# Splitting an expert layer's weights during the attention ahead of it, packing the expert numbers, and 16 places for returned rows

## What is computed

```python
x = x + L0_attn(layernorm(x)); x = x + L0_xattn(layernorm(x), ctx, ctx, mask); x = x + L0_ffn(layernorm(x))
x = x + L1_attn(layernorm(x)); x = x + L1_xattn(layernorm(x), ctx);            x = x + L1_ffn(layernorm(x))
```

```python
Q = (query @ Wq).reshape(b, q_len, G, Hpg, dh) / sqrt(dh);  K = key @ Wk;  V = value @ Wv      # L0_xattn
scores = einsum('bqghd,bkgd->bghqk', Q, K) + m * rel         # masked where mask is false
out = einsum('bghqk,bkgd->bqghd', softmax(scores), V) @ Wo

aff = sigmoid(x @ wa);  p, i = top_k(aff, 2);  p = p / p.sum()                                  # L0_ffn
expert(x) = (gelu(x @ g + gb) * (x @ w1 + b1)) @ w2 + b2     # g, w1: 256 x 128; w2: 128 x 256
y = x + sum over the 2 shared experts + sum over the token's 2 chosen experts of p * expert(x)
```

## Time and profile before

| | |
|---|---|
| median of 3 runs | 2768.86 us (2767.92 to 2770.44) |
| the profiled execution | 2787.7 us, of which the profile shows a span of 2785.9 us |
| busy share of the span | TensorE 74%, VectorE 62%, ScalarE 51%, GpSimd 37% |
| cross attention with its norm | 258 to 475 us |
| norm and routing of the changed expert layer | 475 to 547 us |
| its routed experts | 547 to 694 us |
| shared experts, rows brought back | 694 to 748 us |

### The profile page before, as it was taken

One profiled execution on the slowest core, in us unless ns is written; L12 is line 12 of the kernel. 1 busy time (PEld: TensorE's weight loads), 2 busy tenths in 40 slices (PEclk: granted clock), 3 DMA queues, 4 the chain that ended last, 5 costly groups with the idle time before them and its releaser, 6 DMA issues. The chain is left out here.

```text
span 2785.9 us, 44119 instructions
## 1 busy us (share of the span) xinstructions
PE 2048.7 (74%) x15822; PEld 1226.0 (44%) x15822; DVE 1738.1 (62%) x3146; ACT 1420.1 (51%) x1986; POOL 1018.9 (37%) x920
## 2 busy tenths in 40 slices
PE   6783776156489999999856366666666549999998
PEld 3332554145267777777645122222222234444444
DVE  6996565612533333333365899999999645666665
ACT  4562333412143333333233488888888525666664
POOL 0000221641422322323223588888888600101010
PEclk9996777568789999999967555555555569999999
DMA  3000001576200000000000256666666400000001
GB/s 91 0 0 20 1 0 36 143 143 117 72 20 20 19 19 19 9 19 19 1 23 0 45 107 108 108 108 107 107 107 107 72 18 12 23 24 18 25 17 39
DMA packets 374723, 135.44 MB, mean 49 GB/s; under 512 B 317549, under 2 KB 371525, under 8 KB 374597
## 3 DMA queue, kind: packets, MB, share of 16 engines
q1 hardware_dynamic: 370757, 123.27, 21.8%
q0 software_dynamic: 3840, 10.49, 1.7%
HBM read 47.69 MB, written 10.49 MB: 21 GB/s over the span
## 5 line engine op out<-in xcount | busy, mean ns | idle before, releaser
L2015 POOL CAST xnT<-xl 128x2048 bf16<-128x2048 uint8 x256 | 484.0, 1891 | 15.5
L2050 PE MATMUL psum<-e_KT,e_QT 48*128 48x512 bf16 x1024 | 264.7, 617 | 272.0 <-DVE ctxT L2083 124.9
L2083 DVE TENSOR_SCALAR_CACHE_REDUCE ctxT<-psum,e_nsq 128x1024 f32<-128x1024 f32 x256 | 314.7, 1281 | 11.5 <-PE psum L2050 10.1
L2083 DVE TENSOR_SCALAR_CACHE_REDUCE e_Smore<-psum,e_nsq 128x1024 f32<-128x1024 f32 x256 | 314.7, 1281 | 1.7 <-issue 0.4
L2101 ACT ACTIVATE xh<-e_Smore,e_ebias 128x2048 uint8<-128x2048 f32 x128 | 256.3, 2002 | 48.8 <-POOL e_ebias L2022 48.8
L2101 ACT ACTIVATE xh<-ctxT,e_ebias 128x2048 uint8<-128x2048 f32 x128 | 256.3, 2002 | 47.2 <-POOL e_ebias L2022 47.2
L1563 POOL TENSOR_TENSOR d_sq<-d_oS 128x512 f32<-128x512 f32 x64 | 99.2, 1549 | 420.5 <-ACT d_oS L1607 420.5
L117 PE MATMUL psum<-xh,d_WT 128*128 128x512 f16 x768 | 229.6, 381 | 2.6 <-DVE d_WT L1638 2.6
L2050 PEld LDWEIGHTS psum<-e_KT,e_QT 48*128 48x128 bf16 x1024 | 33.8, 107 | 401.7 <-DVE ctxT L2083 190.1
L1657 DVE TENSOR_TENSOR d_ACC<-psum,d_ACC 128x512 f32<-128x512 f32 x128 | 82.4, 686 | 171.0 <-PE psum L1711 171.0
L2060 PEld LDWEIGHTS psum<-e_Vi,xnT 128*128 128x128 bf16 x4096 | 119.5, 104 | 112.2 <-issue 104.3
(11 more groups left out here) (362 smaller groups left out, 4635.4 us busy)
## 6 DMA issues: line engine op xcount, KB each, us to landing
kept_y<-c_y SPq DMA_DIRECT2D x12, 512.0 KB
d_Wn<-in_L_attn_w_qkv SPq DMA_DIRECT2D x16, 384.0 KB, 3.2
f_W<-in_L_ffn_w_routed SPq DMA_DIRECT2D x32, 176.0 KB, 2.5
xl<-xh SPq DMA_TRANSPOSE x256, 3.0
ctx_rows<-in_ctx SPq DMA_DIRECT2D x1, 2048.0 KB, 8.5
X<-in_x SPq DMA_DIRECT2D x1, 2048.0 KB, 13.9
c_Wgu<-in_L_ffn_rg SPq DMA_DIRECT2D x16, 128.0 KB, 2.6
c_Wgu<-in_L_ffn_rw SPq DMA_DIRECT2D x16, 128.0 KB, 2.6
```

What stands on the lines that cost most here:

```text
L2015: pool.tensor_copy(PT[:, sl, :], P8[:, sl, :, :].rearrange("p c q -> p (c q)").bitcast(U8)).then_inc(unpacked, 1)
L2050: mm = pe.matmul(m.bank[pair_banks(c + odd) + q], QT[rows, n // 2, :], KTt[rows, n % H // 2, col:col + BLK], start=True, stop=True)
L2083: dve.tensor_scalar(S32[sl][:, hf * HALF:(hf + 1) * HALF].rearrange("p (a b) -> p a b", a=2), m.psum[:, b:b + 2, :], nsq[:, n + odd:n + od ...
```

## The change

It does four things.

1. A new class `SplitWeights` holds the split weights and 4 stages for loading. It is made before the cross attention and lives until the expert layer ends. The two shared experts' weights are loaded during the attention's norm and split ahead of its first block. In the block loop, each tile's instructions are followed by the split of one routed expert: four ScalarE instructions behind the tile's last copy, two GpSimd instructions behind the tile's bias. SP reloads a stage when its split is done. The expert layer no longer loads or splits weights, and ScalarE's order there is: square root, first block's high part, biases and gate, other blocks.
2. VectorE packs the four expert numbers of a quad into one word by three more instructions (n3, n2, n1, n0 in base 16), and TensorE loads one word a quad and takes the numbers out of it by shift and mask in registers.
3. `GSLOTS` is 16 instead of 8, and `G` lies in the memory of `xnT`.
4. `GOT` is 2 instead of 3.

```diff
+class SplitWeights:
+    NE, SH, F, SLOTS = 16, 2, 128, 4
...
+    def load(self, sp, kind, e, slot):
+        for part, name in enumerate(("g", "w1")):
+            sp.dma_start(self.Wgu[:, slot, :, part, :],
+                         self.w[f"L0_ffn_{kind}{name}"][e].rearrange("(k p) f -> p k f", p=P)).then_inc(self.w_in[slot], 16)
+        sp.dma_start(self.Wd[:, slot, :], self.w[f"L0_ffn_{kind}w2"][e]).then_inc(self.w_in[slot], 16)
+    def scalar(self, act, e, slot, loads, n):
+        act.wait_ge(self.w_in[slot], 48 * loads)
+        act.activation(self.Wgu[:, slot], self.Wgu[:, slot], ACT.Copy, scale=SPLIT)
+        act.activation(self.Wd[:, slot], self.Wd[:, slot], ACT.Copy, scale=SPLIT).then_inc(self.scaled, 1)
+        act.wait_ge(self.scaled, n + 1)
+        act.activation(self.Wx[:, ds(e, 1), 0].rearrange("p o k a f -> p (o k a f)"),
+                       self.Wgu[:, slot].rearrange("p k a f -> p (k a f)"), ACT.Copy)
+        act.activation(self.WdH[:, ds(e, 1)].rearrange("p o d -> p (o d)"), self.Wd[:, slot], ACT.Copy).then_inc(self.high, 1)
+    def gpsimd(self, pool, e, slot, n):
+        pool.wait_ge(self.high, n + 1)
+        flat = lambda x: self.Wx[:, ds(e, 1), x].rearrange("p o k a f -> p (o k a f)")
+        pool.tensor_tensor(flat(1), self.Wgu[:, slot].rearrange("p k a f -> p (k a f)"), flat(0), ALU.subtract)
+        pool.tensor_tensor(self.WdL[:, ds(e, 1)].rearrange("p o d -> p (o d)"), self.Wd[:, slot],
+                           self.WdH[:, ds(e, 1)].rearrange("p o d -> p (o d)"), ALU.subtract).then_inc(self.split, 1)
@@ gqa_cross_attention, GpSimd @@
+                for slot in range(W.SH):
+                    W.gpsimd(pool, W.NE + slot, slot, slot)
                 pool.wait_ge(prep, 1 + KC * C)
...
                         pool.tensor_tensor(bias[:, tt % 2, :, :], alibi[:, :, :],
                                            neg[:, ds(n, 1), :].broadcast_to((P, NH, SEQ)), ALU.add).then_inc(bias_ready, 1)
+                        W.gpsimd(pool, i * W.SLOTS + tt, tt, i * W.SLOTS + (W.SH + tt))
@@ ScalarE @@
                         if tt:
                             ao_copy(n - 1)
+                        W.scalar(act, i * W.SLOTS + tt, tt, i + (2 if tt < W.SH else 1), i * W.SLOTS + (W.SH + tt))
@@ Dispatch.vector_experts @@
-        dve.tensor_copy(self.expert[:, :], self.te[:, :]).then_inc(self.named, 1)
+        of = self.te[:, :].rearrange("p (q j) -> p q j", j=per)
+        for j in range(per - 2, -1, -1):
+            c.do(dve.scalar_tensor_tensor(self.word[:, :], of[:, :, per - 1] if j == per - 2 else self.word[:, :], float(NE),
+                                          of[:, :, j], ALU.mult, ALU.add))
+        dve.tensor_copy(self.expert[:, :], self.word[:, :]).then_inc(self.named, 1)
@@ experts_top2 @@
-    STAGES, GOT, TURNED, GSLOTS = 6, 3, 3, 8
+    GOT, TURNED, GSLOTS = 2, 3, 16
...
-        G = norm.xn[:, :, :, :].rearrange("p a b d -> p (a b) d")
+        G = m.xnT[:, :, :].rearrange("p a b -> p (a b)").rearrange("p (s d) -> p s d", s=GSLOTS)
...
-                    return [pe.value_load(R.expert[0:1, i:i + 1], min_val=0, max_val=NE - 1)
-                            for i in range(qd * GPQ, (qd + 1) * GPQ)]
+                    word = pe.value_load(R.expert[0:1, qd:qd + 1], min_val=0, max_val=NE ** GPQ - 1)
+                    return [pe.snap((word >> (4 * j)) & (NE - 1)) for j in range(GPQ)]
...
-                pe.wait_ge(split, NE + SH)
```

More of the change, by code:

```diff
@@ L528, in _, with __init__, gqa_cross_attention @@
                 output(NBLK - 1)
-def gqa_cross_attention(nc, m, w):
+class SplitWeights:
+    NE, SH, F, SLOTS = 16, 2, 128, 4
+    def __init__(self, m, w, own):
+        NE, SH, F, SLOTS = self.NE, self.SH, self.F, self.SLOTS
+        self.w = w
+        self.Wgu = m.sb("c_Wgu", [P, SLOTS, KC, 2, F], ctx=own)
+        self.Wd = m.sb("c_Wd", [F, SLOTS, D], ctx=own)
+        self.Wx = m.sb("c_Wx", [P, NE + SH, 2, KC, 2, F], F16, own)
+        self.WdH, self.WdL = (m.sb("c_" + n, [F, NE + SH, D], F16, own) for n in ("WdH", "WdL"))
+        self.scaled, self.high, self.split = (m.sem(f"c_{n}") for n in ("scaled", "high", "split"))
+        self.w_in = [m.sem(f"c_w{i}") for i in range(SLOTS)]
+    def load(self, sp, kind, e, slot):
[17 more added lines that the diff above has]
+                           self.WdH[:, ds(e, 1)].rearrange("p o d -> p (o d)"), ALU.subtract).then_inc(self.split, 1)
+def gqa_cross_attention(nc, m, w, W):
     G, C, HD = 4, 4, 16
@@ L582, in preload, with _ @@
                     load(mask8[b * SEQ:(b + 1) * SEQ, :, :], src.partition_broadcast(SEQ))
+            for slot in range(W.SH):
+                W.load(sp, "s", slot, slot)
         layernorm(nc, m, preload)
         with nc.Block() as block:
+            @block.sync
+            def _(sp):
+                for slot in range(W.SH):
+                    sp.wait_ge(W.split, slot + 1)
+                    W.load(sp, "r", slot, slot)
+                for slot in range(W.SH, W.SLOTS):
+                    W.load(sp, "r", slot, slot)
+                with sp.Fori(1, NBLK) as i:
+                    for slot in range(W.SLOTS):
+                        sp.wait_ge(W.split, i * W.SLOTS + (W.SH - W.SLOTS + 1) + slot)
+                        W.load(sp, "r", i * W.SLOTS + slot, slot)
             @block.gpsimd
             def _(pool):
+                for slot in range(W.SH):
+                    W.gpsimd(pool, W.NE + slot, slot, slot)
                 pool.wait_ge(prep, 1 + KC * C)
@@ L596, in _ @@
                                            neg[:, ds(n, 1), :].broadcast_to((P, NH, SEQ)), ALU.add).then_inc(bias_ready, 1)
+                        W.gpsimd(pool, i * W.SLOTS + tt, tt, i * W.SLOTS + (W.SH + tt))
             @block.scalar
             def _(act):
+                for slot in range(W.SH):
+                    W.scalar(act, W.NE + slot, slot, 1, slot)
                 act.wait_ge(prep, 1 + KC * C)
@@ L952, in __init__ @@
         self.te = sb("te", [P, self.groups])
-        self.expert = sb("expert", [P, self.groups], U32)
+        self.word = sb("word", [P, tiles // TPB])
+        self.expert = sb("expert", [P, tiles // TPB], U32)
         self.slot, self.tile, self.row = (sb(n, [P, NT, top]) for n in ("slot", "tile", "row"))
@@ L1186, in _ @@
                     norm.sync(sp, b)
[L1187 to L1191, removed]
                 sp.wait_ge(bias_split, 3)
@@ L1278, in take @@
                                    ACT.Copy).then_inc(evac_act, 1)
-                split_high(0)
-                split_high(1)
                 norm.scalar_sd(act)
[L1283 to L1287, removed]
+                norm.scalar_high(act, 0)
                 act.wait_ge(loaded, 16 * NLOADS)
@@ L1290, in _ @@
                 R.scalar_gate(act, R.wa[:, :, :].rearrange("p k e -> p (k e)"))
+                for b in range(1, NBLK):
+                    norm.scalar_high(act, b)
                 R.scalar_scores(act, m.bank[6])
-                for n in range(STAGES + 2, NE + SH):
-                    split_high(n)
                 act.wait_ge(tables, 1)
@@ L2423, in build @@
         rotary_recurrence(nc, m, {**own, "freq": w["freq"], "mean_w": w["mean_w"]})
-        gqa_cross_attention(nc, m, w)
         kept_rows = nc.dram_tensor("kept_rows", (TOK, 2 * D), F16, kind="Internal").ap()
         kept_y = nc.dram_tensor("kept_y", (C_SLOTS, D), F32, kind="Internal").ap()
-        with m.stage():
-            experts_top2(nc, m, w, kept_rows, kept_y)
+        with m.stage(), ExitStack() as split:
+            W = SplitWeights(m, w, split)
+            gqa_cross_attention(nc, m, w, W)
+            experts_top2(nc, m, w, W, kept_rows, kept_y)
         lightning_attention(nc, m, w)
```

40 lines of the change are left out of this document (5 added, 35 removed).

## The result

The changed kernel takes 2805.07 us (median of 4 runs, 2802.65 to 2807.93), the kernel before 2768.41 us on the same chip (2767.92 to 2770.44). The ratio is 1.0131, 95% interval 1.0114 to 1.0149: 36.7 us slower. The prediction said 2792, slower, range 2764 to 2816.

A forecast was written before the change was run, and what follows sets the result against it. No engine was full: attention, norm and routing, and routed experts were chains of waits, with a tail behind. +74 - 16.5 - 33 - 1 = +23.5 us, carried over to the median 2768.86, gave 2792 us, range 2764 to 2816.

The forecast's parts named there:

- Attention, +74: Cross attention: GpSimd's next bias pass queues behind its wait for ACT's split; steps 13.9 instead of 7.64 us, +74 us.
- Rival C: Cross attention: the bias pass doesn't become part of the step, so the splits are hidden; -50, 2718 us; chance 0.05.
- Norm and routing, -16.5: Norm and routing without splits: earlier square root, VectorE free of GpSimd's work, earlier row transposes; -16.5 us.
- Routed experts, -33: Routed experts: one register load a quad instead of four, two places for gathered rows; 114 us instead of 147, -33.
- 114 predicted: Routed experts' new length: 20 us start, ten quads of 8.0, 9 for last products, 5 until rows are written.
- I take 8.0: Routed experts: time per quad in us, set by gathers waiting for transposes with two places; TensorE itself needs 5.8.
- The 1.1 us a load: Routed experts: price of each of four register loads, read from TensorE's 4.53 us gap before a quad's down products.
- Rival A: Routed experts: TensorE, not the gather loop, sets the quads, from about 6 us each; -54, total 2763 us; chance 0.12.
- Tail, -1: Shared experts and rows brought back: sixteen places shrink GpSimd's waits, but gathers don't end the stage; -1 us.
- The 7.3 us: Tail: a VectorE wait the profile doesn't explain, read as an engine stopping while a long run of gathers is issued.
- the 12.5 us: Tail: GpSimd's 32 gathers' wait for VectorE's combining, expected to shrink with sixteen places.
- I carry the difference over: Whole kernel: the +23.5 us summed on the profiled execution is added to the runs' median, 2768.86, giving 2792 us.

The follow-up runs named there:

- e1: The changed kernel with GpSimd's order in each attention block made bias 0, 1, 2, split 0, bias 3, split 1, 2, 3; 2712.16 us.
- e4: The kernel before, unchanged, run once more for a second profile; its profiled execution took 2766.57 us.
- e7: The changed kernel with GpSimd doing 18 splits' subtractions once more during norm and routing; 2820.35 us.
- e2: The kernel before with the packed expert numbers alone, one register load a quad instead of four; 2745.23 us.
- e5: The changed kernel with three places for gathered rows instead of two; 2803.58 us.
- e3: The kernel before with 16 places for rows brought back instead of 8, and nothing else; 2767.76 us.
- e8: e1 and e5 together, with GpSimd's bias pass released by the subtraction of two tiles before instead of its scale-and-bias; 2703.70 us.

## Why the prediction was right, and where it wasn't

1. *Attention, +74*: right in mechanism and size (+74.1). The steps of 14.1 us, the two waits and the subtraction at 1.22 are in the rows, and e1 shows that GpSimd's order alone makes them. Rival C ("the attention hides its splits") is what e1 is.
2. *Norm and routing, -16.5*: right (-16.8), by its parts too. Against e4 the square root is 2.3 us earlier (2.2 predicted), the norm behind it 3.6 shorter (3), the rest up to the choice of experts 2.4 (3, put to SP), the routing chain 8.5 (8.3). e7 shows the chain's cause; ACT's and SP's parts were not tested.
3. *Routed experts, -33*: this is the step that failed. Its new length was nearly right (114 predicted, 117.1 measured), but was subtracted from the 147 us of one execution, 14 us more than e4's 133.1. And the length was right by luck, since it came from a wrong mechanism: "*I take 8.0*" for the gather loop, with TensorE needing 5.8. It was TensorE, at 7.6: the register instructions ahead of a quad's up products take 4.7 us to issue. The prediction has no term for those that make addresses, and 0 for the shifts and masks (some 0.7 of the 4.7), because these "stand between matmuls that wait for the array anyway"; but the products wait for the issuing. The 2.84 us of the earlier trace rows hid this: the 32 register instructions of that row took 4.0 us too (608.84 to 612.88), but the first ran 1.57 us ahead of the first up product, while the down products before it ran at only 0.21 us each. The 1.1 us a load came from the longest of the ten gaps of that profile (4.53 us); those of e4 are 2.93 to 3.80. Rival A named the right engine at the wrong price. Of the -16, the packed numbers make -21 (e2); two places instead of three give back 3 to 5 (e5, e2).
4. *Tail, -1*: right (0, e3). The 7.3 us and most of the 12.5 us belong to the odd execution too. By the Trainium skill's rule ("Runtime: NRT & Kernel Launch", Instruction fetch mechanics), that crossing into the next block of instructions costs little, the tail was to lose 10 us. Ten of eleven profiles have no such stop, but e4 of the kernel before is among them, and so nothing was gained. What the stops of the one execution were, no run here shows. The same section's 200 ns for a register load doesn't fit e4: the 48 loads of its routed stretch take 0.29 to 1.02 us each in the trace, 0.54 in the mean, and four leave gaps of 2.9 to 3.8 us.
5. *"I carry the difference over"*: the profiled execution was 18.8 us above the median, and I took the sum over to the median without asking where that excess lay. It lay in stretches that the change works on, so the -33 counts part of it as a gain. The trace had signs of it: seven "issue" gaps of TensorE among one quad's down products, 6.6 us together, and 7.3 us "remote". With the stretches of e4 the same steps give 74 - 16.5 - 19 - 1 = +37.5, so 2806; measured 2805. That it comes so close is luck again, since the 114 us in the -19 were right by luck.

## What to carry to other kernels

Work given to an idle engine is not free if it waits there: look at what is queued behind the wait, and put the waiting work behind what others need soon (93 us between the changed kernel and e1, with the same instructions). Where a profiled execution is longer than the median, find the place of the excess before taking a difference from any stretch. A duration read from products that were issued ahead is a lower bound; once a gap is closed, the issuing shows, and each register instruction between the products counts.

## What was not expected of the hardware

- TensorE products behind a register instruction that makes their address start 124 ns apart in e5, and a shift or mask in a register takes 97 ns of the same queue; 48 products with constant addresses take 2.84 us (59 ns each) at a granted clock of 1.00. Where the registers set the pace, 64 products took 6.6 us at 0.75 and at 1.00 alike.
- One of eleven profiled executions was 24 us longer than the next of the same kernel in two stretches, 14 in the routed experts and 10 in the tail, beside long runs of indirect gathers. 6.6 us in seven gaps of TensorE and one wait of 7.3 us of VectorE are plain in its trace.
- How much a GpSimd pass costs the VectorE instruction beside it: 1.1 us on a subtraction of 1024 columns (1.22 to 2.32), and as much as 0.9 on one of 16 (0.17 to 1.06), since it waits for the pass, whatever its own length. Moving the bias passes off them brought the attention's 16 subtractions from 35.2 us (e4) to 20.2 (e8): 15 of the 24 us by which e8's attention is shorter than that of the kernel before, with more work in it.
